# A second attention whose heads use 64-row tiles, two heads per maxima unit, in one unrolled plan

## What is computed

```
x = x + attention(layernorm(x), Wq, Wk, Wv, Wo)

q = rope(heads(x @ Wq.T));  k = rope(heads(x @ Wk.T));  v = heads(x @ Wv.T)   # 16 heads of 16 columns
scores = where(causal, (q @ k.T) / 16, -huge)                                 # 2048 x 2048 for each head
out = softmax(scores) @ v                                                     # then @ Wo.T
```

## Time and profile before

| | |
|---|---|
| time, median of 3 runs | 2342.56 us (2339.42 to 2347.28) |
| profiled execution | 2343.61 us, span 2341.8 us |
| TensorE busy over the span | 2037.0 us (87%) |
| VectorE, ScalarE, GpSimd busy | 1676.4, 1000.3, 975.4 us |
| second attention's heads | 1651 to 2286 us from the span's start |

### The profile page before, as it was taken

How to read it: one execution, slowest core, us unless ns; L and a number is a source line. 1 busy time by engine, 2 the same in 40 slices (tenths; PEclk the granted TensorE clock), 3 DMA queues, 4 the chain that set the end, 5 groups by cost and what they waited for, 6 DMA issues and landing times. The chain is left out here.

```text
span 2341.8 us, 36616 instructions
## 1 busy us (share of the span) xinstructions
PE 2037.0 (87%) x10632; PEld 1205.8 (51%) x10632; DVE 1676.4 (72%) x3188; ACT 1000.3 (43%) x2042; POOL 975.4 (42%) x865
## 2 busy tenths in 40 slices
PE   4757999999999999999999999567699998999996
PEld 3634555555555555555555554455454554554545
DVE  6667877878778778687787784775586785767825
ACT  1223343443434434434434434111167666666771
POOL 0023685795775856956957766013300000000000
PEclk8867999999999999999999999678799999999998
DMA  2200000000000000000000000110000000000001
GB/s 84 65 8 5 8 1 5 9 1 5 8 1 12 1 5 8 1 5 8 1 5 0 1 1 0 39 39 23 1 1 1 1 1 1 2 2 1 1 1 37
DMA packets 19790, 23.26 MB, mean 10 GB/s; under 512 B 4128, under 2 KB 17952, under 8 KB 19488
## 3 DMA queue, kind: packets, MB, share of 16 engines
q1 hardware_dynamic: 18416, 20.00, 2.8%
q10 hardware_dynamic: 1200, 1.31, 0.2%
HBM read 19.21 MB, written 2.10 MB: 9 GB/s over the span
## 5 line engine op out<-in xcount | busy, mean ns | idle before, releaser
L1100 ACT ACTIVATE lath_probs<-lath_shifted 128x512 f32<-128x512 f32 (+3 forms) x640 | 357.8, 565 | 683.3 <-DVE lath_shifted L1211 650.5
L1177 POOL TENSOR_TENSOR lath_summed<-lath_summed,lath_probs 128x512 f32<-128x512 f32 (+3 forms) x528 | 584.6, 1128 | 122.4 <-ACT lath_probs L1100 112.4
L1211 DVE TENSOR_TENSOR lath_shifted<-lath_score,lath_shift 128x512 f32<-128x512 f32 (+3 forms) x640 | 385.3, 607 | 147.8 <-PE lath_score L986 131.5
L1218 DVE TENSOR_REDUCE lath_maxima<-lath_max 128x1 f32<-128x512 f32 (+3 forms) x640 | 380.3, 605 | 132.4 <-PE lath_max L1007 84.8
L1623 DVE TENSOR_REDUCE atth_maxima<-atth_max 128x1 f32<-128x512 f32 (+3 forms) x640 | 355.1, 605 | 98.2 <-PE atth_max L1746 54.2
L1702 ACT ACTIVATE atth_probs<-atth_score 128x512 f32<-128x512 f32 (+3 forms) x640 | 313.6, 536 | 178.4 <-PE atth_score L1760 92.0
L994 PE MATMUL lath_out<-lath_probs,lat_latent 128*64 128x512 f32 (+3 forms) x1280 | 307.2, 559 | 0.0
L1007 PE MATMUL lath_max<-lat_key_hi,lath_query_hi 128*128 128x512 f32 (+3 forms) x640 | 266.0, 424 | 18.0 <-DVE lath_maxima L1218 16.5
L1746 PE MATMUL atth_max<-atth_key,atth_query 128*128 128x512 f32 (+3 forms) x640 | 267.3, 429 | 15.1 <-DVE atth_query L1595 6.2
L982 PE MATMUL lath_score<-lath_query_hi,lat_key_hi 128*128 128x512 f32 (+3 forms) x640 | 265.9, 415 | 4.0 <-DVE lath_shifted L1211 4.0
L1760 PE MATMUL atth_score<-atth_query,atth_key 128*128 128x512 f32 (+3 forms) x640 | 246.6, 407 | 14.0 <-ACT atth_probs L1702 11.6
(11 more groups left out here) (341 smaller groups left out, 2839.3 us busy)
## 6 DMA issues: line engine op xcount, KB each, us to landing
ffn_a_w<-in_L_ffn_W SPq DMA_DIRECT2D x2, 1024.0 KB, 11.7
lat_raw_out<-in_L_attn_w_out SPq DMA_DIRECT2D x8, 256.0 KB, 2.7
lat_rope<-in_c_rope_feature SPq DMA_DIRECT2D x1, 2048.0 KB, 10.8
ffn_b_w<-in_L_ffn_W SPq DMA_DIRECT2D x2, 1024.0 KB, 7.6
mix_a_factors<-in_L_ffn_factors SPq DMA_DIRECT2D x8, 256.0 KB, 4.1
out<-x SPq DMA_DIRECT2D x4, 512.0 KB, 2.9
lat_raw_q<-in_L_attn_w_q_b SPq DMA_DIRECT2D x8, 192.0 KB, 2.4
x<-in_L_attn_x ACTq DMA_DIRECT2D x2, 512.0 KB, 7.0
```

The costliest lines, as they stand in the source:

```text
L1100: nc.scalar.activation(probs[:, prob_slot(j, kt), h, q0:CH], shifted[:, 2 * (kt % 2) + h, q0:CH], ACT.Exp, scale=SCALE0).then_inc(s["exp_d ...
L1177: last = nc.gpsimd.tensor_tensor(summed[:, j % 2, h, q0:CH], so_far, probs[:, prob_slot(j, kt), h, q0:CH], ALU.add)
L1211: nc.vector.tensor_tensor(shifted[:, 2 * (kt % 2) + h, q0:CH], score_bank[score_place(j, kt, h) % 3][:, q0:CH], shift[:, j % 2, h, q0:CH], ...
L1218: nc.vector.reduce_max(maxima[:, h, i, kc:kc + 1], max_bank[(i * (nj + 1) + kc) % 2][:, 0:width], AX.X).then_inc(s["maxima_taken"], 1)
```

## The change

The three parts of the stage keep their interfaces, and the numbers computed are the same. Inside `attention_heads`:

- Each matmul for maxima or scores takes only its own head's 64 rows of keys and queries (`rows_of(h)`). The zeroed halves of `query` and their memsets are gone. A `query` tile now holds two heads.
- A maxima job is for two heads (a pair) and fills a **slot** of two banks, one for each head; there are two slots in place of three maxima banks and the side bank. One reduction reads both banks. Diagonal tiles are regrouped: `triangle` (the four masked 128-wide tiles side by side, the mask of 4 x 128 written first by one matmul per head), `odd` (128 and 384 columns) and `even` (256). A pair and chunk has `3 + 4 j` jobs, 288 in the stage.
- The turns of keys, queries and shifted queries take both pairs at once (eight transposes) through the same two slots, as do the finishes. The shift is made once for four heads.
- Diagonal score tiles get their mask as before, by a matmul of 128 rows behind the score.
- All four groups are written out in one plan (`attention_plan`). It gives each event a due time from a step time of 2.45 us and a cost of each maxima job, and sorts. Maxima, turns and finishes share one order, which alternates the two slots. The last group's chunks run in the order 3, 2, 1, 0.
- `key` and `v_one` have two copies, one for even and one for odd groups. GpSimd copies the values and the high parts; ScalarE empties the turned queries, VectorE the turned keys.

In steps with maxima, the usual order on TensorE is score 0, a maxima job, scores 1 and 2, a maxima job, score 3, values.

The core of the diff:

```diff
-FINISH_AT = (3.8, 2.95, 3.3, 2.85)
-MAXIMA_STEPS = [(-11.1, -8.55), (-6.9, -0.4), (-0.5, 9.7), (9.4, 22.8)]
...
+QUERY_TILES = 4
+STEP_TIME = 2.45
+LAST_GROUP = NCH * (NG - 1)
+CHUNKS = [(g, j) for g in range(NG - 1) for j in range(NCH)] + [(NG - 1, j) for j in reversed(range(NCH))]
+
+def maxima_jobs(j):
+    for pair in range(2):
+        yield pair, "triangle", 0, ((0, CH),)
+        yield pair, "odd", 0, ((1, P), (3, 3 * P))
+        yield pair, "even", 0, ((2, 2 * P),)
+        for i in range(TPC):
+            for kc in range(j):
+                yield pair, "whole", kc, ((i, CH),)
+
+def attention_plan():
+    jobs, others, step_ends = [], [], []
+    maxima_end = step_end = 0.0
+    ended = []
+    for n, (g, j) in enumerate(CHUNKS):
+        begin = max(maxima_end, ended[n - QUERY_TILES] + 3.0 if n >= QUERY_TILES else 0.0)
+        others.append((begin - 6.0, ("split_queries", n)))
+        jobs.append((begin - 1.3, 1.2, ("queries", n)))
...
+        at = begin
+        for k, job in enumerate(maxima_jobs(j)):
+            jobs.append((at, 0.0, ("maxima", n, k, *job)))
+            at += 0.18 * len(job[3]) + sum(width for _, width in job[3]) / 480
+        maxima_end = at
+        jobs.append((at + 1.6, 1.2, ("shifted", n)))
+        step_end = max(step_end, at + 4.5)
         for kt in range(key_tiles(j)):
...
+            length = STEP_TIME * (0.2 + 0.8 * (CH - max(kt - TPC * j, 0) * P) / CH)
+            others += [(step_end + 0.25 * h * length, ("scores", n, kt, h, len(step_ends))) for h in range(GROUP)]
...
-        v_one = sb("v_one", [P, NT, GROUP, 32])
-        key = sb("key", [P, 2, TOKENS], F32R)
-        query = sb("query", [P, NCH, GROUP, CH], F32R)
+        v_one = sb("v_one", [P, 2, NT, GROUP, 32])
+        key = [sb(f"key{n}", [P, 2, TOKENS], F32R) for n in range(2)]
+        query = sb("query", [P, QUERY_TILES, 2, CH], F32R)
...
-        max_bank = [ctx.enter_context(nc.psum_tensor(f"atth_max{i}", [P, CH], F32)) for i in range(3)]
+        slot = [ctx.enter_context(nc.psum_tensor(f"atth_slot{i}", [P, 2, CH], F32)) for i in range(2)]
         out_bank = ctx.enter_context(nc.psum_tensor("atth_out", [P, CH], F32))
-        side_bank = ctx.enter_context(nc.psum_tensor("atth_side", [P, CH], F32))
...
+                def turn(r, slots, n):
+                    for pair in range(2):
+                        for i in range(TPC):
+                            last = nc.tensor.transpose(slot[r % 2][:, pair, i * P:(i + 1) * P], slots[:, n % 2, i, 2 * pair:2 * pair + 2, :]
+                                                       .rearrange("p h c -> p (h c)"), core.ident)
+                    last.then_inc(s["filled"], 1)
...
+                    if kind in ("maxima", "keys", "queries", "shifted", "finish") and a[0] >= 2:
+                        wait_taken(pe, a[0] - 2)
...
+                        if what == "triangle":
+                            for h in range(2):
+                                nc.tensor.matmul(slot[r % 2][:, h, :], core.ident_b, core.mask_qk.unsqueeze(1).broadcast_to([P, TPC, P]),
+                                                 start=True, stop=False)
+                            for i in range(TPC):
+                                for h in range(2):
+                                    own = slice(j * CH + i * P, j * CH + (i + 1) * P)
+                                    last = nc.tensor.matmul(slot[r % 2][:, h, i * P:(i + 1) * P],
+                                                            query[rows_of(h), n % QUERY_TILES, pair, i * P:(i + 1) * P],
+                                                            key[g % 2][rows_of(h), pair, own], start=False, stop=(i == TPC - 1))
+                        else:
+                            begin = 0
+                            for i, width in parts:
+                                first = (kc if what == "whole" else j) * CH
+                                for h in range(2):
+                                    last = nc.tensor.matmul(slot[r % 2][:, h, begin:begin + width],
+                                                            query[rows_of(h), n % QUERY_TILES, pair, i * P:(i + 1) * P],
+                                                            key[g % 2][rows_of(h), pair, first:first + width], start=True, stop=True)
+                                begin += width
+                        last.then_inc(s["filled"], 1)
...
+                        wait(pe, s["exp_done"], u - 2)
+                        q0 = queries_from(kt, j)
+                        mm = nc.tensor.matmul(score_bank[u % 3][:, q0:CH], key[g % 2][rows_of(h), h // 2, kt * P:(kt + 1) * P],
+                                         query[rows_of(h), n % QUERY_TILES, h // 2, q0:CH], start=True, stop=(kt < TPC * j))
+                        if kt >= TPC * j:
+                            mm = nc.tensor.matmul(score_bank[u % 3][:, q0:q0 + P], core.ident_b, core.mask_kq, start=False, stop=True)
+                        mm.then_inc(s["scores_done"], 1)
...
+                            nc.vector.reduce_max(maxima[:, n % 2, heads, :, 0], slot[r % 2][:].rearrange("p h (t k) -> p h t k", t=TPC), AX.X)\
+                              .then_inc(s["taken_by_vector"], 1)
...
+                                nc.vector.reduce_max(maxima[:, n % 2, heads, i, at], slot[r % 2][:, :, begin:begin + width], AX.X)\
+                                  .then_inc(s["taken_by_vector"], 1)
...
+                    elif kind in ("queries_out", "shifted_out"):
+                        r, = a
+                        act.wait_ge(s["filled"], r + 1)
+                        nc.scalar.activation(query[:, n % QUERY_TILES], slot[r % 2][:], ACT.Copy).then_inc(s["taken_by_scalar"], 1)
```

More of the change, by code:

```diff
@@ L1409, in placed_events @@
-def placed_events():
-    placed = []
-    for j in range(NCH):
-        alone, turns = preparation(j)
-        placed += [(step, j, [(step, event)]) for step, event in alone] + [(turn[0][0], j, turn) for turn in turns]
-    for j in range(-1, NCH - 1):
-        step = STEPS_BEFORE[j + 1] + FINISH_AT[j + 1]
-        placed.append((step, j, [(step, ("finish", j))]))
-    placed.sort(key=lambda p: p[0])
-    out, side_end = [], -KT_PER_PAIR
-    for step, j, together in placed:
-        if together[0][1][0].startswith("turn") or together[0][1][0] == "finish":
-            late = max(side_end - step, 0)
-            side_end = together[-1][0] + late + 0.01
-            together = [(at + late, event) for at, event in together]
-        out.append((step, j, together))
-    return out
@@ L1458, in attention_prologue @@
-def attention_prologue():
-    placed = [e for step, _, together in placed_events() if step < 0 for e in together]
-    return [event for _, event in sorted(placed, key=lambda e: e[0])]
-ATTENTION_EPILOGUE = ([("values", -1, key_tiles(NCH - 1) - LAG + i, half) for i in range(LAG) for half in range(2)]
-                      + [("drain", -1), ("finish", -1)])
-VECTOR_PLACES = (0, 1)
-SIDE_PER_GROUP = 7 * NCH
-SIDE_BEFORE = sum(e[0].startswith("turn") for e in attention_prologue()) - 1
-def with_side_uses(events, start, earlier):
-    out, uses = [], dict(earlier)
-    for e in events:
-        kind, j, *rest = e
-        if kind == "place":
-            e = (*e, uses[e[1:4]])
-        elif kind.startswith("turn") or kind == "finish":
-            if kind != "finish":
-                uses[kind, j, rest[0]] = start
-            e, start = (*e, start), start + 1
-        elif kind == "split":
-            e = (*e, uses.get(("turn_shifted", j - 2, 1)))
-        elif kind == "maxima":
-            e = (*e, uses["turn_queries", j, rest[0] // 2])
-        elif kind == "scores":
-            e = (*e, uses["turn_shifted", j, rest[1] // 2])
-        out.append(e)
-    return out, start, uses
@@ L1498, in attention_heads @@
+MAXIMA_JOBS = [len(list(maxima_jobs(j))) for j in range(NCH)]
+TAKEN_BY_SCALAR = ("queries", "shifted")
 def attention_heads(core, qk, v, attended):
     nc = core.nc
-    prologue, _, uses = with_side_uses(attention_prologue(), -SIDE_BEFORE, {})
-    first, _, uses = with_side_uses(attention_schedule(True, False), 1, uses)
-    uses = {(kind, j - NCH, pair): use - SIDE_PER_GROUP for (kind, j, pair), use in uses.items()}
-    middle, _, _ = with_side_uses(attention_schedule(False, False), 0, uses)
@@ L1505, in attention_heads @@
-    final, side_end, _ = with_side_uses(attention_schedule(False, True), 0, uses)
-    epilogue, _, _ = with_side_uses(ATTENTION_EPILOGUE, side_end - SIDE_PER_GROUP, {})
+    plan = attention_plan()
+    jobs = {e[2]: e[0] for e in plan if e[0] in ("maxima", "keys", "queries", "shifted", "finish")}
+    place = {e[:2]: e[2] for e in plan if e[0] in ("keys", "queries", "shifted", "finish")}
+    reads = {"keys_out": 1, "queries_out": 1, "shifted_out": 1, "maxima": 1, "finish_out": 2}
+    counts, read = {}, {True: 0, False: 0}
@@ L1507, in attention_heads @@
+    for e in plan:
+        if e[0] in reads:
```

(4 more changed lines are left out.)

445 lines of the change are left out of this document (183 added, 262 removed).

## The result

The changed kernel takes 2457.24 us (median of 4 runs, 2454.63 to 2462.48), the kernel before 2344.04 us beside it: ratio 1.0487, 95% interval 1.0461 to 1.0513. It is 113 us slower where 60 us less was forecast. The profiled execution has a span of 2452.8 us at a mean granted clock of 0.883, before 2341.8 us at 0.934.

A forecast was written before the change was run, and what follows sets the result against it. TensorE was taken to bound the second attention's stage (576 of 635 us busy). Terms -22 - 45 - 5 + 46 + 14 + 10 - 20 - 38 = -60 took 2343.6 to 2284 us, range 2255 to 2315, chance 0.50.

The forecast's parts named there:

- Waits, -38: TensorE's 60 us of waits in the second attention's stage would shrink to 22, with two double banks and shifts planned ahead.
- the waits stay: Rival: late turns and maxima hold each other up in two shared slots, 60 us of waits; 2322, up to 2345; chance 0.21.
- Head, -20: Stage start before the first score: 56 us becomes 31, some 5 of the 25 saved returning as later maxima.
- Scores of full steps -22: In 96 full steps, scores 1 and 2 run together on different rows, so four TensorE slots become three: -22 us.
- full-width maxima -45: 384 full-width maxima matmuls become 192 pairs on different rows and banks, overlapping fully at 0.233 us: -45 us.
- chain +10: Full steps with maxima: TensorE's 2.36 us falls below the unchanged 2.61 us latency chain, giving back 21 us, turns filling about half.
- Pairs do not overlap: Rival: 64-row matmuls on different rows follow one another; 2352 us, slower than before by 0.4%; chance 0.13.
- Diagonal scores, +46: 256 masked score units mix 64-row scores with 128-row masks, changing tile form twice, +0.18 us each: +46 us.
- turn and finish +14: 128-row transposes between 64-row work add two tile-form changes each: +11 us for 48 turns, +3 for 16 finishes.
- Tile changes are free: Rival: switching between 64-row and 128-row matmuls costs nothing, so the +46 and +14 vanish; 2224 us; chance 0.16.
- VectorE and ScalarE at nothing: Reductions, exponentials and copies on these engines add no time, covered by TensorE's work; uncovered, ScalarE's copies could show 10 us.

The follow-up runs named there:

- pad4_both: Changed kernel with all score and maxima matmuls on 128 rows, four query tiles, keys' slot and turned output single: 2433.17 us, ratio 1.0380.
- old_scores64: Kernel before the change, old order kept, only the score matmuls reading 64 rows, maxima on 128: 2562.53 us, ratio 1.0899.
- pad_maxima: Changed kernel with zero-padded queries, three query and `probs` tiles, maxima matmuls on 128 rows, scores on 64: 2638.24 us, ratio 1.1269.
- pad_scores: Changed kernel with zero-padded queries, three query and `probs` tiles, score matmuls on 128 rows, maxima on 64: 2492.60 us, ratio 1.0619.

## Why the prediction was wrong

**The sum had no term for the clock.** Every duration was taken from rows at a granted clock of 1.00 and carried over to code that uses the array differently. This is the step that failed most: +112 us by the split above, where work and idle time together give -12. That reading 64 rows in place of 128 lowers the clock was shown twice: alone in the old order (19 to 285 us lost), and taken back in the new order (188 to 53). The runs with added full-array work point the same way, by less. The rows are not the whole of it: pad4_both, the new order on 128 rows, loses 58 us. As an estimate from these traces, some 73 of the 112 us go with the rows (131 less 58) and some 39 with the new order (58 less 19). Why the new order costs clock, and what in a 64-row matmul does it, stays open. The Trainium skill (TensorE: Matmul & The Clock Gate, Part 1) has the throttle released by activity, and the clock falling when the engine is idle. The trace agrees with that in the head, where TensorE is busy for 19.68 of 33 us and is at 0.52; it differs in the tail, where TensorE is busy for 38.72 of 39 us at 0.50, and the measurement decides.

**Waits, -38.** Wrong in sign. I took 22 us of idle time for 60; it became 94. The rival "the waits stay" named the mechanism, turns and maxima holding each other up in two slots, but its upper end, 2345 us, stands for no more than 83 us of idle time. The sign that was named for being wrong, TensorE idle for VectorE in the middle of the groups, came too: of the stage's idle time 25.5 us end with VectorE's copy of turned keys and 32.8 with ScalarE's of turned queries. The sum counted a turn as TensorE's own time and covered the copy with other work; in a first-in-first-out of two slots nothing lies between a turn, its copy and the maxima that need it.

**Head, -20.** The first score came 33 us after the stage's start, 31 were forecast. But the first group then pauses for 19, 15 and 19 us, and it ends no earlier. The windows over the first group, before and after:

```profile
1651.00:1860.00 209.00, 177.46 (x1044) 101.29 (x1048) 145.80 (x299) 115.67 (x246) 17.07 (x21) 0.91 0.00 1
```
```profile
1648.00:1887.00 239.00, 197.26 (x1102) 101.33 (x1102) 141.09 (x168) 104.94 (x204) 22.23 (x43) 0.80 0.00 1
```

At full clock that is 209 x 0.91 = 190 and 239 x 0.80 = 191 us: nothing was gained. The same maxima have to come before the last scores of the group; I had 5 us coming back, it was all.

**Scores of full steps -22, full-width maxima -45, chain +10.** Right: pairs start together and take 0.22 to 0.24 us, and a full step with maxima takes 2.60 us at full clock. "Pairs do not overlap" fell, and with it the one rival that forecast a slower kernel, for another reason.

**Diagonal scores, +46 (turn and finish +14).** Near: in the tail a unit of 512 columns costs 0.23 us more than before (0.59 for 0.36), I had 0.18. Where a slot job on 64 rows runs ahead of it, it takes 0.49 (0.33 from score to mask, 0.42 in the tail). Over all units at full clock the medians of the four widths are 0.13 to 0.23 us above before's, 0.20 on the mean, so 256 of them are about +51. "Tile changes are free" fell. TensorE's work at full clock fell by 43 us where my terms for it, from the scores of full steps to the finishes, come to -12; as ends of matmuls are modelled, the split can't say which of them was too dear.

**VectorE and ScalarE at nothing.** Right for their work (369 and 364 us), wrong for the copies, as above.

Of the signs I had named, the pairs, the step of 2.6 us and the first score after some 31 us came as described, wherever the clock was 1.00; the masked unit came at 0.59 or 0.49 for 0.54 and the stage at 744 for 575. That the kernel came out slower, as one rival had it, speaks for nothing in that rival.

## What to carry to other kernels

Before halving the rows of a matmul to run two side by side, look for what the array does when it does not run two: here the scores stood mostly alone or between masks, and the granted clock went from 0.96 to 0.79. A zero half can be the cheaper form: with it the old order took 2344 us, without it 2620. And multiply each window's length by its granted clock before comparing stages: one glance at 588 against 610 would have told the clock from the schedule.

When several kinds of work share a few banks in one fixed order, count each kind's whole stay in the bank (fill, copy, hand-over back), and expect that a wait taken from one of them shows up at the next.

## What was not expected of the hardware

- A TensorE that was busy for 38.72 of 39 us ran at a granted clock of 0.50, with 64-row scores, 128-row masks and 32-column values.
- The last 16 steps, the same instructions, ran at 1.00 in one kernel (40 us) and at 0.50 in another (62 us).
- With one or two superfluous 128-row matmuls of 512 columns in each step the mean clock over the span rose, from 0.88 to 0.89 and 0.90 or more, in all four runs of each.
- In the old order, alternating 64-row and 128-row matmuls in full is dearer than either form: 688 us of work at full clock in old_scores64, 580 with both kinds on 64 rows, 560 with both on 128. In the new order this holds for pad_maxima (610 against 510 and 565), not for pad_scores (552), where two 64-row maxima of a pair still run together.
